# The causal mask of the row maxima moved from a fused VectorE operation to a bf16 matmul, in an attention loop that is written out

## What is computed

```
scores = einsum('bhsd,bhtd->bhst', q, k) * scale
scores = where(causal, -inf, scores)        # causal: keys behind the query's own place
probs  = softmax(scores, axis=-1)
out    = einsum('bhst,bhtd->bhsd', probs, v)
```

## Time and profile before

| what | us |
|---|---|
| median of 3 runs | 1605.16 (1602.48 to 1610.64) |
| the profiled execution, its own time | 1608.4 |
| its span in the trace | 1606.7 |
| PE busy in the span | 1381.6 (86%) |
| DVE busy | 1139.5 (71%) |
| ACT busy | 860.6 (54%) |

### The profile page before, as it was taken

One profiled execution on the slowest core, in us unless ns is written; L12 is line 12 of the kernel. 1 busy time (PEld: TensorE's weight loads), 2 busy tenths in 40 slices (PEclk: granted clock), 3 DMA queues, 4 the chain that ended last, 5 costly groups with the idle time before them and its releaser, 6 DMA issues. The chain is left out here.

```text
span 1606.7 us, 27137 instructions
## 1 busy us (share of the span) xinstructions
PE 1381.6 (86%) x8384; PEld 821.8 (51%) x8384; DVE 1139.5 (71%) x2689; ACT 860.6 (54%) x1155; POOL 229.9 (14%) x206
## 2 busy tenths in 40 slices
PE   5988888750799999999999989999999976899997
PEld 5877777640443343343343333433433422799986
DVE  5666676821788888877887887888888930567675
ACT  5644444310036666655665665666666655466564
POOL 0012222346001011010010110110110101110100
PEclk9999999875568899997997999999999978899999
DMA  5113333437152062070080260440620002222312
GB/s 204 40 40 105 105 118 100 150 123 95 13 69 34 6 83 24 5 101 8 9 98 5 30 82 5 55 52 6 72 34 5 8 8 68 92 80 92 95 51 66
DMA packets 101898, 97.86 MB, mean 61 GB/s; under 512 B 46288, under 2 KB 85200, under 8 KB 100048
## 3 DMA queue, kind: packets, MB, share of 16 engines
q1 hardware_dynamic: 101744, 95.98, 29.0%
HBM read 57.15 MB, written 37.75 MB: 59 GB/s over the span
## 5 line engine op out<-in xcount | busy, mean ns | idle before, releaser
L1001 ACT ACTIVATE probs<-s_ps 128x1024 f32<-128x1024 f32 (+3 forms) x640 | 542.7, 895 | 327.7 <-PE s_ps L1133 326.4
L1112 PE MATMUL m_ps<-kT,qT 64*128 64x512 f32 (+3 forms) x1280 | 478.9, 478 | 112.9 <-DMA qT<-qkT_parts 55.9
L1026 DVE TENSOR_REDUCE maxes<-m_ps 128x1 f32<-128x512 f32 x768 | 490.8, 684 | 48.5 <-PE m_ps L1112 44.2
L1112 PEld LDWEIGHTS m_ps<-kT,qT 64*128 64x128 f32 x1280 | 217.2, 201 | 502.2 <-DVE maxes L1026 274.0
L1133 PE MATMUL s_ps<-qT,kT 64*128 64x512 f32 (+3 forms) x1280 | 327.3, 416 | 13.8 <-DMA qT<-shiftT 10.5
L1031 DVE CUSTOM_DVE_ANT_0 masked<-m_ps,mask_b 128x384 f32<-128x384 f32 (+3 forms) x512 | 238.3, 488 | 130.6 <-PE m_ps L1112 125.0
L1150 PE MATMUL o_ps<-probs,v_w 128*32 128x512 f32 (+3 forms) x2560 | 322.4, 578 | 0.2 <-POOL probs L974 0.2
L974 POOL TENSOR_SCALAR_AFFINE_SELECT probs<-probs 128x512 f32<-128x512 f32 x128 | 81.6, 637 | 851.8 <-ACT probs L1001 851.8
L1133 PEld LDWEIGHTS s_ps<-qT,kT 64*128 64x128 f32 x1280 | 164.2, 198 | 41.0 <-ACT probs L1001 25.0
L313 ACT ACTIVATE relu_a<-ups_a 128x512 f32<-128x512 f32 x64 | 38.1, 596 | 100.8 <-PE ups_a L562 99.9
L1150 PEld LDWEIGHTS o_ps<-probs,v_w 128*32 128x32 f32 x2560 | 51.9, 111 | 76.5 <-issue 58.9
(11 more groups left out here) (124 smaller groups left out, 1917.7 us busy)
## 6 DMA issues: line engine op xcount, KB each, us to landing
kT<-qkT_parts SPq DMA_DIRECT2D x48, 256.0 KB
qT<-qkT_parts SPq DMA_DIRECT2D x96, 128.0 KB
qkT_parts<-qk_hi_a SPq DMA_DIRECT2D x32, 256.0 KB, 3.0
qkT_parts<-qk_lo_a SPq DMA_DIRECT2D x32, 256.0 KB, 3.4
qT<-shiftT SPq DMA_DIRECT2D x512, 1.0 KB
xin_a<-in_x SPq DMA_DIRECT2D x8, 512.0 KB, 4.0
xres_a<-in_x SPq DMA_DIRECT2D x8, 512.0 KB, 4.9
x<-xsum_a SPq DMA_DIRECT2D x8, 512.0 KB, 3.2
```

The lines of the kernel that those rows point to most:

```text
L1001: act.activation(probs[:, b % PBUF, 2 * hp:2 * hp + 2, off:CH], s_ps[hp][:, :, off:CH], ACT.Exp, scale=D ** -0.5)\
L1026: dve.tensor_reduce(out, m_ps[:, bank, 0:width], AX.X, ALU.max).then_inc(max_read, 1)
L1112: pe.matmul(m_ps[:, bank, 0:width], qT[of % 2][r0:r0 + HR, j, h // 2, t * P:(t + 1) * P], kT[of % 2][r0:r0 + HR, h // 2, k * CH:k * CH + w ...
```

## The change

The loop is written out for all 8 groups, so no register stands in a wait. `find` becomes `unit`, with the same matmul; for a masked unit a second matmul follows into the same bank, with the identity as weights and the 128 x 128 mask as the moving operand, both in bf16, K = 128. DVE runs the plain maximum for every unit. The negated maxima are no longer transposed by DVE but by PE, as an item of the ring of its own (`turn_shift`, a 128 x 32 transpose), four units behind the last unit of the chunk; DVE copies them to SBUF (`shift_out`), and SP carries them in 4 DMAs of 4 KB in place of 16 of 1 KB. `att` has two buffers. SP issues the loads of the next group one term at a time, in slots 0 to 11, in place of three lots at the starts of chunks 0, 1 and 2.

```
-        mask = sb("mask_b", [P, CH])
-        masked = sb("masked", [P, 2, CH])
+        mask = sb("mask_b", [P, P])
+        maskb, identb = sb("maskb", [P, P], BF16), sb("identb", [P, P], BF16)
...
+            for n in range(GROUPS):
+                for j in range(NJ):
+                    last = max(i for i, (_, e) in enumerate(order) if e[0] == "unit" and e[1] == n and UNITS[e[2]][0] == j)
+                    after = [i for i, (_, e) in enumerate(order) if i > last and e[0] == "unit"][:4]
+                    at = after[-1] if after else last
+                    order.insert(at + 1, (order[at][0], ("shift", n, j)))
...
-            with eng.Fori(0, PAIRS - 1) as i:
-                for dn, j in turn:
-                    body(i, dn, j, False)
...
-                        for r in range(P // VW):
-                            c0 = VW * r + G * T * a + G * T // 2 * par
-                            sp.dma_start(out[:, :, r, :].bitcast(F32), shiftT[c0:c0 + G * T // 2, :]).then_inc(shift_in, 16)
+                        row, c0 = HR * par + KR + a, G * T * a + G * T // 2 * par
+                        out = qT[n % 2][row:row + 1, j, :, :].rearrange("o h (t q) -> o (h t) q", t=T)
+                        sp.dma_start(out.bitcast(F32), shiftT[c0:c0 + G * T // 2, :]).then_inc(shift_in, 16)
...
-                if k < j:
-                    dve.tensor_reduce(out, m_ps[:, bank, 0:width], AX.X, ALU.max).then_inc(max_read, 1)
-                else:
-
-                    dve.wait_ge(max_read, done - 1)
-                    dve.sem_inc(passed_max, 1)
-                    dve.tensor_tensor_reduce(masked[:, u % 2, 0:width], m_ps[:, bank, 0:width], mask[:, CH - width:CH], 1.0, NEG,
-                                             ALU.add, ALU.max, out).then_inc(max_read, 1)
+                dve.wait_ge(max_done, i + 1)
+                dve.tensor_reduce(maxes[:, j % 2, par, hp, t, k:k + 1], m_ps[:, i % MB, 0:width], AX.X, ALU.max).then_inc(max_read, 1)
...
+            def shift_out(e):
+                i = ITEM[e]
+                dve.wait_ge(max_done, i + 1)
+                wait(dve, shift_in, SHIFTS * step_no(e[1], e[2]))
+                dve.tensor_copy(shiftT[:, :], m_ps[0:2 * G * T, i % MB, 0:P]).then_inc(max_read, 1)
...
+                mm = pe.matmul(m_ps[:, i % MB, 0:width], qT[n % 2][r0:r0 + HR, j, hp, t * P:(t + 1) * P],
+                               kT[n % 2][r0:r0 + HR, hp, k * CH:k * CH + width], start=True, stop=True)
+                if k == j:
+                    mm = pe.matmul(m_ps[:, i % MB, t * P:(t + 1) * P], identb[:, :], maskb[:, :],
+                                   start=False, stop=True, skip_group_check=True)
+                mm.then_inc(max_done, 1)
+
+            def turn_shift(e):
+                i = ITEM[e]
+                free_bank(i)
+                pe.wait_ge(neg_step, 3 * step_no(e[1], e[2]) + 3)
+                pe.transpose(m_ps[0:2 * G * T, i % MB, 0:P], negparts[:, :, :].rearrange("p a c -> p (a c)"), ident[:, :])\
                   .then_inc(max_done, 1)
```

More of the change, by code:

```diff
@@ L939, in _ @@
+            moves(BLOCKS * GROUPS)
+            for p in range(2):
+                sp.wait_ge(att_out[p], 16 * NJ * GROUPS // 2)
         @block.gpsimd
@@ L1184, in _, with ring @@
-            pe.wait_ge(const_in, 32)
-            for x in range(MAX_FROM, 0):
-                for u in unit_slots[x]:
-                    find(0, 0, x, 0, u)
-            steps(pe, body)
+            def ring(items):
+                for e in items:
+                    if e[0] == "unit":
+                        unit(e)
+                    elif e[0] == "shift":
+                        turn_shift(e)
+                    else:
+                        turn_sums(e)
+            pe.wait_ge(mask_ok, 2)
@@ new lines, in _ @@
+            for g in range(MAX_FROM, 0):
+                ring(ITEMS.get(g, []))
+            slots = [(n, j, b) for n, j in steps() for b in range(T * j + T)]
+            for g, (n, j, b) in enumerate(slots):
+                items = ITEMS.get(g, [])
+                units = sum(e[0] == "unit" for e in items)
+                q = [units * quarter // 4 for quarter in range(4)]
+                ring(items[:q[1]])
+                scores(n, j, b, 0)
+                ring(items[q[1]:q[2]])
+                scores(n, j, b, 1)
+                ring(items[q[2]:q[3]])
+                if g >= 2:
+                    products(*slots[g - 2])
+                ring(items[q[3]:])
@@ L1191, in build @@
+            for slot in slots[-2:]:
+                products(*slot)
+            ring(ITEMS[BLOCKS * GROUPS])
 def build(nc, x, w, out):
```

473 lines of the change are left out of this document (184 added, 289 removed).

## The result

The changed kernel takes **1681.45 us** (median of 4 runs, 1672.33 to 1691.72) against 1603.82 us before (4 runs, 1601.5 to 1610.64): ratio **1.0478**, interval 1.041 to 1.0547. It is slower, inside the range forecast (1670 to 1880), but by 78 us and not by 170.

The account below looks back on a forecast made before the run. PE was taken as the bound: masks 229 plus transposed maxima 30, less 88 of slack, show +171; prelude +21, loop -13 and SP -12 make +167, about 1775 us. Forecast 1720 to 1840; wider range 1670 to 1880.

Parts of the forecast that it names:

- The bound: Attention groups: PE has 5 to 16 us of slack a group, 12 taken; whatever it gets beyond lengthens the group.
- DVE's gain: Plain in place of fused maxima drop 42 us of accumulator reads, yet give 0 us, bounds -10 and 0.
- the 120 named: Sign in the groups: the prediction is wrong if they take under 120 us though masks don't follow units within 0.1.
- The mask's price: A mask on PE between 64-row work costs 0.51 us, bounds 0.36 and 0.6; all masks together 229 us of PE time.
- What a group makes disappear: PE's slack absorbs 12 us of the 35 added to each group, 88 of 259 in all, so +171 shows.
- rival B: Slack takes all it can and reloads were due anyway: slower by less, about 1685 us; chance 0.16.
- rival C: Emptying leaves PE not streaming, a third of some 950 us at half clock: 72 us more, 1850 and above; chance 0.17.
- The transposes and SP: 32 PE transposes of the maxima cost +30 us, from 20 to 40; four DMAs at the last chunk give -12.
- Prelude: 44 masked units at half clock, 0.96 us each on PE against some 0.48 on DVE: +21 us, bounds 10 and 30.
- The rest of the change: Outside the masks: transposed maxima +30, loop stops gone -13, SP's fewer DMAs -12; spread loads and second `att` buffer 0.
- The rule against this price: At some 81 ns a load and matmul, the 468 masks outside the prelude would be 38 us and vanish in slack.
- what would show it: Profile signs: mask load 0.21 us after its unit's columns, DVE waits 0.8 a slot, groups 130 to 136 us, prelude about 69.

Follow-up runs that it names:

- nomask: The changed kernel without the mask matmul on PE, DVE's plain maxima kept and also seeing masked keys; 1543.69 us, ratio 0.9611 to the kernel before.
- fused: The changed kernel without the mask matmul, DVE adding the mask in its fused maximum as before the change; 1546.1 us, ratio 0.9631 to the kernel before.
- dveshift: The changed kernel, masks on PE, with DVE's block transpose of the maxima and 16 DMAs a chunk put back; 1668.88 us, ratio 1.0398.
- loop_only: fused with DVE's block transpose of the maxima and 16 DMAs a chunk put back; 1576.7 us, ratio 0.9818 to the kernel before.
- fused_vfirst: fused with the loads of v and the rows of ones ahead of those of q and k in the prelude; 1549.64 us, ratio 0.9645.
- twice: The changed kernel with two mask matmuls, each of half the value, behind every masked unit; 1669.82 us, ratio 1.039 to the kernel before.

## Why the prediction was right and where it was wrong

- **The bound: right.** PE was the engine to watch; what it got beyond its slack showed. DVE's gain, forecast at 0, is 0 (nomask against fused). The size was wrong, and by the prediction's own sign: a group at full clock takes 116 us, under the 120 named, though masks don't follow their units within 0.1.
- **The mask's price: the step that failed.** The step read 0.21 us of "emptying" from a unit to the first transpose and to the products, and then added 0.10 for a reload. But the unit's own open weight load was inside the 0.21, so the 0.10 stood in the sum twice, and the load and way back of the bf16 identity is 0.11 beside its columns, not 0.15. It measured 0.37 in place of 0.51: the lower bound, 0.36, whose condition was named ("the reload was due anyway, and bf16 loads fast"), was the value. For 342 masks that is 48 us of the 229. Before products 0.18 is near the 0.2 taken.
- **What a group makes disappear: taken as 12 us, measured as 17.6, and not all of it is slack.** By the measured prices a group holds 47 masks x 0.37 + 17 x 0.18 + 2.3 for broken pairs (the forecast's figure, not measured) + 4 transposes x 0.6 = 25 us more PE work, forecast 35. It is 7.6 longer than before. But 2.3 of what disappears is a gain that the sum had at 0: without masks the rest of the change makes a group shorter, 106.0 against 108.3, although its four transposes are in it. From fused to after the masks add 22.8 us of work to a group and 9.9 show, so 13 are absorbed, close to the 12. The waits agree: the loads of units wait 117 us less for DVE in after than in before, 17 a group, and 76 less than in fused (316), 11 a group.
- **The two together** made 23 us a group of what is 7.6. This is rival B, "the slack takes all it can and the reloads were due anyway", priced at 1685 and given 0.16. Its price and its condition on the reloads came true; what it says of slack holds beside before, with the gain of the rest in it.
- **The clock: rival C in part, at a fraction of its size.** The forecast counted half clock only as a surcharge of 13 us. After loses 50 us above its full-clock groups, before 31.5. C had 72 us more for a third of the time at half clock; it was 18.5 for a mean of 0.91 against 0.93 in groups 0 to 6. Beside fused, which has almost none of it, it is near 50. Where it would fall (the sixteen masked units of chunk 0 in a row) the prediction did not say.
- **The transposes and SP:** +30 and -12 stood for a loss of 18. With masks on PE the swap measured 12 (dveshift), near it, but with both terms smaller: in the traces at most 2.5 us in each of seven groups, and 7 gained in group 7. Without masks the same edit is worth -31, which no step foresaw: a term of a sum holds only beside the others.
- **Prelude:** +8.2, not +21. Two masked units of 256 columns stand 0.99 and 0.72 us apart in it (start of one to start of the next, 419.43, 420.42, 421.14), and where no bank was waited for, 0.72, the forecast's terms make 0.90. Most of the difference is the way from the mask to the next unit, 0.22 (420.92 to 421.14), for which they have 0.36 (0.1 + 0.11 + 0.15). That PE gets ahead during plain units, where DVE is the slower one, is argued only.
- **The rest of the change: the other step that failed.** The sum has the masks at +162 (229 - 88 + 21) and all else at +5 (30 - 13 - 12). By fused it is 135 and -58. Taken in the other order, loop_only and dveshift give -29 for the loop and the loads (forecast -13), 92 for the masks (162) and 12 for the transposes (18). The two splits differ since the masks fill waits that loop_only has and fused has not (the scores' wait for DMAs, over 4 us a group). The loop's stops went, as forecast; that the groups would keep the clock without masks, no step says. The -10.3 before the first unit had been put at 0: 4.4 of it lie between the first large load and the first unit (2.5 of it seen in fused_vfirst), and 5.9 came before the first large load, in a phase that the change does not touch.
- **The rule against this price** (the Trainium skill, TensorE: Matmul & The Clock Gate, Back-to-back issue gap, 81 ns for each load and matmul of 128 columns) does not fit here: a mask between 64-row work measured 0.37 us. Within one layout it is close: the second mask of twice starts 0.07 us behind the first. The Trainium skill, TensorEngine Tiling (Array Packing), Key Properties, has a change of tiling mode drain the engine; the rows agree, with 0.11 us of it.

Of what would show it: read as the prediction reads it, the weight load of a mask starts 0.21 us after the columns of its unit, and the next 64-row load 0.16 behind, both as named; the sign could not show that 0.10 of the 0.21 was a load already counted. Units wait less for DVE, as said. DVE's waits for units are 0.68 us a slot over groups 0 to 6, where 0.8 or more was named, and 0.45 before. Groups take 116 to 126 us, not 130 to 136; the stop is gone and the last chunk's scores wait for no DMA, only 1.5 us of PE for DVE's parts, as this row of the waits of after, 1316 to 1409 us, has it:

```profile
PE m_ps L1010 <- DVE negparts L943: 1.5, 1, 1.5
```

## What to carry to other kernels

- Moving work from an engine with a little slack to the one that has less is paid twice where the moved work runs in another layout of the array: a mask is cheap on TensorE as two K = 64 matmuls among K = 64 work (16 us for 512 masks, 0.03 us each in the end), and dear as one K = 128 matmul between them (135 us, 0.26 us each, with what the clock takes).
- When a gap between two instructions is priced, say for each 0.1 us of it which load, stream or drain it holds, before a second term is added for the same thing.
- Look for the places where the clock falls before the change too. Here they were the same in every group, and work added there cost more than its own time.
- A change of several parts wants each part tried beside the others: here the part that was not the point gave 58 us, the one that was cost 135, and an edit that was worth 31 us alone cost 12 beside the masks.

## What the hardware showed that was not expected

- A change of layout empties PE for 0.11 us at full clock (805.11 to 805.37 less load and columns; 630.35 to 630.50 less columns), and a bf16 identity of 128 x 128 with its 128 columns takes 0.16 to the next piece.
- More matmuls can be faster: 128 added where pieces of two layouts alternate took 23 us off, and the clock stayed at 2.4 GHz in places where it had fallen to 1.2 for up to 31 us (PEclk 0.52 over 631 to 662 us in after), with PE read as 95 to 100% busy in both.
- On VectorE the fused add and maximum with its read of the accumulator costs no more time than the plain maximum in this loop, though its busy time is 83 ns higher each.
